# The third convolution of a token stage with its input as the stationary operand and 256 moving weight columns, and the last token norm folded into the output weights

## The reference, cut to what matters

```python
def tok(x):                                             # [b, 128, 64, 3]
    h = layernorm(x.reshape(b, t, j * 3), ln0_g, ln0_b).reshape(b, t, j, 3)
    h = relu(conv2d(h, conv1_w, conv1_b, ((2, 2), (1, 1))))
    h = layernorm(h.reshape(b, t, j * 3), ln0_g, ln0_b).reshape(b, t, j, 3)
    h = relu(conv2d(h, conv2_w, conv2_b, ((2, 2), (0, 0))))
    h = layernorm(h.reshape(b, t, j * 2), ln1_g, ln1_b).reshape(b, t, j, 2)
    h = relu(conv2d(h, conv3_w, conv3_b, ((2, 2), (0, 0))))   # 128 -> 256 token channels, 5 x 2 taps
    h = h.reshape(b, 2 * t, j)
    res = concatenate([h[:, :t, :], h[:, t:, :]], axis=2)     # [b, 128, 128]
    return layernorm(res, ln1_g, ln1_b) @ out_w + out_b       # -> [b, 128, 64]
# then: h + attention(layernorm(h)), whose logits are, for 8 heads and all pairs of the 128 tokens,
#   -sum_w |q[s, h, w] - k[t, h, w]| / 8                      over 64 w
# then: h + experts(layernorm(h)), one of 32 small experts for each token
```

## Time and profile before

| | before |
|---|---|
| median of 3 runs | 3468.23 us (3464.18 to 3468.46) |
| the profiled execution | 3481.97 us, span from first to last instruction 3480.2 us |
| PE busy | 3227.9 us (93%) |
| DVE busy | 3130.7 us (90%) |
| POOL busy | 2849.9 us (82%) |
| ACT busy | 2577.4 us (74%) |

### The profile page before, as it was taken

The page is one execution under the profiler, slowest core; times in us unless marked ns, Lnnn a source line. Parts: engine busy times, 40 slices in busy tenths (PEclk is TensorE's granted clock), DMA queues, the critical chain, the costliest instruction groups (busy, mean ns, idle before and its releaser), DMA issues. The chain is left out here.

```text
span 3480.2 us, 78005 instructions
## 1 busy us (share of the span) xinstructions
PE 3227.9 (93%) x23116; PEld 2461.7 (71%) x23116; DVE 3130.7 (90%) x4358; ACT 2577.4 (74%) x4378; POOL 2849.9 (82%) x2728
## 2 busy tenths in 40 slices
PE   8899999999999999999999999999999999999888
PEld 6677777776777777777777777767777777777655
DVE  5899999999999999999999999999999999999876
ACT  3777787777777777777777777777777777777763
POOL 3788888888888888888888888888888888888874
PEclk9999999999999999999999999999999999999988
DMA  6778777778777778777777777787777787777773
GB/s 136 152 156 161 154 158 158 153 154 166 155 152 158 153 153 166 156 156 153 156 157 158 157 157 154 154 165 153 157 158 153 155 163 157 155 155 153 157 152 70
DMA packets 199652, 534.96 MB, mean 154 GB/s; under 512 B 69142, under 2 KB 133398, under 8 KB 150968
## 3 DMA queue, kind: packets, MB, share of 16 engines
q0 software_dynamic: 73728, 492.86, 71.4%
q1 hardware_dynamic: 125880, 41.54, 5.9%
HBM read 10.93 MB, written 2.10 MB: 4 GB/s over the span
## 5 line engine op out<-in xcount | busy, mean ns | idle before, releaser
L925 DVE TENSOR_REDUCE S<-psU 128x16 f32<-128x1024 f32 x2216 | 2629.9, 1217 | 235.4 <-PE psU L487 220.9
L487 PE MATMUL psU<-flat,kT 99*128 99x256 bf16 x16384 | 2291.6, 275 | 189.9 <-DVE S L925 119.4
L712 ACT ACTIVATE absd<-psU 128x1024 f32<-128x1024 f32 x1880 | 1913.4, 1023 | 587.0 <-PE psU L487 575.9
L487 PEld LDWEIGHTS psU<-flat,kT 99*128 99x128 bf16 x16384 | 1498.0, 98 | 832.1 <-DVE S L925 316.8
L1183 POOL TENSOR_TENSOR absd<-absd 128x1024 f32<-128x1024 f32 (+2 forms) x512 | 1183.5, 2312 | 111.3 <-DMA absd<-absd 110.1
L1189 POOL TENSOR_TENSOR absd<-absd 128x512 f32<-128x512 f32 (+4 forms) x768 | 767.5, 999 | 60.2
L1171 POOL DMA_DIRECT2D absd<-absd x512 | 454.0, 887 | 244.8 <-ACT absd L712 186.2
L499 PE MATMUL psC<-c1in,w 128*128 128x384 f32 (+1 forms) x930 | 314.3, 421 | 17.0 <-DVE c1in L969 16.9
L591 PE MATMUL psZ<-P,v 128*128 128x256 f32 x1024 | 279.1, 379 | 0.0
L936 DVE TENSOR_REDUCE S<-absd 128x64 f32<-128x512 f32 (+4 forms) x512 | 264.3, 516 | 1.3 <-POOL absd L1189 1.3
L518 PE MATMUL psC<-c3in,w 128*128 128x128 f32 x1240 | 245.8, 282 | 1.7 <-DVE c3in L969 1.7
(11 more groups left out here) (180 smaller groups left out, 2266.8 us busy)
## 6 DMA issues: line engine op xcount, KB each, us to landing
absd<-absd POOLq DMA_DIRECT2D x379, 1024.0 KB, 8.1
absd<-absd POOLq DMA_DIRECT2D x98, 768.0 KB, 6.5
flat<-qparts SPq DMA_DIRECT2D x3072, 8.0 KB, 4.0
absd<-absd POOLq DMA_DIRECT2D x35, 512.0 KB, 4.6
xin<-in_x SPq DMA_DIRECT2D x32, 192.0 KB, 6.4
flat<-pattern SPq DMA_DIRECT2D x4, 768.0 KB, 10.9
out_h<-result SPq DMA_DIRECT2D x32, 64.0 KB, 6.1
w<-in_w SPq DMA_DIRECT2D x1, 1280.0 KB
```

The source lines that it names most:

```text
L487: mm = nc.tensor.matmul(psU[:, slot % PLACES, m], kT[0:ROWS + 3, b, m, :], flat[0:ROWS + 3, half % HALVES, :, lo:lo + BLOCK], start=True, ...
L712: nc.scalar.activation(absd[:, c % GROUPS, :, u], psU[:, slot % PLACES].rearrange("p (n a) s w -> p n (a s w)", n=2), ACT.Abs).then_inc(a_ ...
L925: nc.vector.tensor_reduce(S[:, b, hd, SB * c:SB * c + SB], psU[:, slot % PLACES].rearrange("p a s w -> p s a w"), AX.XY, ALU.add, apply_ab ...
```

## The change

The operands of the third convolution swap roles. The input of a tap, c3in with the batch as its innermost dimension (64 positions x 2 batches = 128 columns), becomes the stationary operand, and the weights of both halves are the 256 moving columns: 10 matmuls, and one bf16 matmul of three rows that adds the bias, which the lead-in splits into three bf16 parts. So the convolution's output has its (position, batch) on the partitions. ACT applies relu and writes SBUF (res); PE transposes res back for the statistics and at the same time multiplies it by `wcentre`, which holds the output weights times gain, less their mean over the features, for each batch separately. What is left of the norm is one factor per token: DVE forms h = product x rstd + constant in two operations, one for each batch. ACT's norm, its gain and shift, and POOL's two products go. The positions change too: conv3 is spread over slots 76, 78, 81, 84, 86, 89, 92, 95, 97 and 100, its bias matmul stands at 103, relu at 106, transposes and product together at 111, statistics at 113, and h at 119. In the lead-in the smaller loads of gain, shift and output weights become twelve DMAs, and DVE makes the bias rows (`weigh_out`) and the folded weights (`fold`).

```diff
-TOK_ACT = Steps("copy relu1 relu2 relu3a relu3b norm0 norm1 turned")
+TOK_ACT = Steps("copy relu1 relu2 relu3")
...
-TOK_POOL = Steps("vara rstda varb rstdb varc rstdc vard rstdd meand shiftd")
+TOK_POOL = Steps("vara rstda varb rstdb varc rstdc vard rstdd")
...
-TOK_AT = dict(copy=3, a=7, conv1=14, len1=22, b=47, conv2=56, len2=10, c=67, conv3=76, len3=33, d=112, turn=121,
-              out=126, root=0, gap=4)
+TOK_AT = dict(copy=3, a=7, conv1=14, len1=22, b=47, conv2=56, len2=10, c=67, conv3=76, len3=30, d=113, turn=111,
+              out=118, root=0, gap=4)
...
+        for b in range(2):
+            for hf in range(2):
+                here, there = slice(b, T, 2), slice(hf * J, hf * J + J)
+                weights += [(ln1g_col[here, hf:hf + 1], a["ln1g_col"][there, :]),
+                            (ln1b_col[here, hf:hf + 1], a["ln1b_col"][there, :]), (wout[here, hf, :], a["wout"][there, :])]
...
-                for n in spread(slot, TOK_AT["conv3"], TOK_AT["len3"], 20):
+                for n in spread(slot, TOK_AT["conv3"], TOK_AT["len3"], 11):
...
-                    hf, m = n // 10, n % 10
-                    dy, dx = m // 2, m % 2
-                    mm = nc.tensor.matmul(z[:, 0:2 * T].rearrange("p (b a j) -> p b a j", b=2, a=2)[:, :, hf, :],
-                                          w3[:, m, hf * T:hf * T + T], c3in[:, :, dy:dy + J, dx],
-                                          start=(m == 0), stop=(m == 9))
...
+                    if n < 10:
+                        mm = nc.tensor.matmul(z[:, 0:2 * T], c3in[:, n % 2, n // 2:n // 2 + J, :].rearrange("p j b -> p (j b)"), w3[:, n, :],
+                                              start=(n == 0), stop=False)
+                    else:
+                        nc.tensor.matmul(z[:, 0:2 * T], ones_row[:, :], b3rows[:, :], start=False, stop=True).then_inc(by_pe, 1)
                 if slot == TOK_AT["turn"]:
-                    pe.wait_ge(by_act, TOK_ACT.after(q, "norm1"))
-                    for b in range(2):
-                        mm = nc.tensor.transpose(z[:, b * T:b * T + T], resn[:, b, :], ident[:, :])
+                    pe.wait_ge(by_act, TOK_ACT.after(q, "relu3"))
+                    for hf in range(2):
+                        mm = nc.tensor.transpose(z[:, hf * T:hf * T + T], res[:, hf, :], ident[:, :])
                     mm.then_inc(by_pe, 1)
-                if slot == TOK_AT["out"]:
-                    pe.wait_ge(by_act, TOK_ACT.after(q, "turned"))
-                    for b in range(2):
-                        mm = nc.tensor.matmul(z[:, b * LAT:b * LAT + LAT], resT[:, b, :], wout[:, :],
-                                              start=True, stop=True)
+                    for hf in range(2):
+                        mm = nc.tensor.matmul(z[:, 2 * T:2 * T + 2 * LAT], res[:, hf, :], wcentre[:, hf, :],
+                                              start=(hf == 0), stop=(hf == 1))
                     mm.then_inc(by_pe, 1)
...
+                    if name == "c":
+                        to = c3in[:, :, 2:2 + J, b].rearrange("p w j -> p j w")
+                        y = z[:, b * n:b * n + n].rearrange("p (j w) -> p j w", w=2)
+                        nc.vector.scalar_tensor_tensor(to, y, rstd[name][:, b:b + 1],
+                                                       bb[:, :].rearrange("p (j w) -> p j w", w=2),
+                                                       ALU.mult, ALU.add).then_inc(by_dve, 1)
+                        continue
...
-                    nc.vector.tensor_tensor(h[:, :, :], z[:, 0:2 * LAT].rearrange("p (b w) -> p b w", b=2),
-                                            bout[:, :, :], ALU.add).then_inc(by_dve, 1)
+                    dve.wait_ge(by_pool, TOK_POOL.after(q, "rstdd"))
+                    for b in range(2):
+                        nc.vector.scalar_tensor_tensor(h[:, b, :], z[:, 2 * T + b * LAT:2 * T + b * LAT + LAT],
+                                                       rstd["d"][:, b:b + 1], cout[:, :], ALU.mult, ALU.add).then_inc(by_dve, 1)
```

More of the change, by code:

```diff
@@ L658, in first @@
                         pe.wait_ge(ones, ONES)
+                        pe.wait_ge(split, 7)
+                    if s == TOK_AT["conv3"] + TOK_AT["len3"]:
+                        pe.wait_ge(folded, 4)
+                        for n, w in enumerate((wgain, wshift)):
+                            for hf in range(2):
+                                mm = nc.tensor.matmul(psZ[:, n * LAT:n * LAT + LAT], average[:, :], w[:, hf, :],
+                                                      start=(hf == 0), stop=(hf == 1))
+                        mm.then_inc(averaged, 1)
+                    if s == TOK_AT["turn"]:
+                        pe.wait_ge(folded, 11)
                     tok(0, s, psL, lead_pe, lead_act, lead_dve)
@@ L1001, in tok @@
                 if slot == TOK_AT["d"]:
[L1002 to L1003 removed]
+                    dve.wait_ge(by_pe, TOK_PE.after(q, "out"))
+                    stats(z[:, 0:2 * T].rearrange("p (f b) -> p b f", b=2), "d", by_dve, after("d"))
                 if slot == TOK_AT["out"] + 1:
@@ L1113, in first @@
                         dve.wait_ge(ones, ONES)
-                    if s == TOK_AT["out"]:
-                        dve.wait_ge(loaded, LOADED)
+                    if s == TOK_AT["turn"] - 1:
+                        fold()
                     tok(0, s, psL, lead_pe, lead_act, lead_dve, lead_pool)
+                    if s == TOK_AT["c"] + TOK_AT["gap"]:
+                        weigh_out()
                     if s == TOK_AT["a"] + TOK_AT["gap"]:
```

103 lines of the change are left out of this document (65 added, 38 removed).

## The result

| | before | after |
|---|---|---|
| median | 3468.35 us (4 runs, 3464.18 to 3473.89) | 3495.86 us (4 runs, 3493.28 to 3497.04) |
| profiled execution | 3481.97 us, span 3480.2 | 3493.28 us, span 3491.4 |
| PE, DVE, ACT, POOL busy | 3227.9, 3130.7, 2577.4, 2849.9 us | 3221.0, 3145.9, 2525.8, 2836.1 us |

The change makes the kernel slower (ratio 1.0074, 95% interval 1.006 to 1.0087); the medians lie 27.5 us apart where 25 were forecast. The sum came out right; of its larger parts only h did, and one part was missing.

A forecast was written before the change was run, and what follows sets the result against it. No engine is full; PE and DVE nearly are and hold each other, so DVE's read of slot 127 counts. 0.72 us a pair over 30 iterations (21.6) plus 3.7 lead-in make 25: 3468.2 + 25 = 3493 us, range 3460 to 3508.

The forecast's parts named there:

- reads late through slots 86 to 97 and the rows for slot 116: Convolution matmuls in the PE-bound stretch delay DVE's reads, so SP sends slot 116's rows later: 0.25 us a pair.
- h behind slot 119: Two DVE operations in a stretch without a pause, where one was free in the seam's gap: 0.42 us (0.35 to 0.5).
- strided c3in: DVE's writes to c3in with 8-byte steps between columns cost 0 to 0.22 us more a pair; 0.05 taken.
- steady iteration: Three per-pair terms, 0.25 + 0.42 + 0.05 = 0.72 us, lengthen the iteration from 105.4 to 106.1 us.
- lead-in: Before the first unit: weight operations on DVE and the order delay h of pair 0; net 3.7 us (1 to 8).
- sum: Whole execution: 21.6 us over 30 iterations and 3.7 in the lead-in, 25 us slower.
- The convolution on PE: Twenty 0.23 us matmuls (4.6 us) become ten of 0.44 (4.4) plus a bias matmul: PE gains nothing worth counting.
- The step to slot 116: Rows land 0.25 us later; 0.7 to 0.85 us of transposes and product stay covered by the 1.05 us DMA wait.
- rival (b): Strides to c3in cost their upper end: 5 us more, 3498, or 3505 with the statistics' reads; chance 0.08.
- frees nothing: Work PE loses behind slots 121 and 126 gives no time back, since DVE has no pause there.
- (d): Relief pays: ACT's 1.5 us and PE's 0.64 shorten DVE's waits by 0.5 to 0.7 us a pair; 3468, chance 0.17.
- A premise: Iteration 30, without token stage, still takes 105.0 us, so work taken out of the token stage comes back as waiting.

The follow-up runs named there:

- experiment 2: Changed kernel with the two operations for h moved back behind slot 127, the product left where the change put it: 3509.74 us, ratio 1.0124.
- experiment 4: Changed kernel with weights laid out by the host, 9 transfers instead of 19 and none of single elements: 3502.29 us, ratio 1.01.
- Experiments 5 to 7: 5: kernel before, output product cut to one column, 3496.79 us; 6: changed kernel, product and h back at the seam, 3484.85; 7: changed kernel, zero matmuls there, 3492.4.
- the second profile of the kernel before: The kernel before, unchanged, run and profiled again: 3468.75 us, ratio 1.0007, its profiled execution 3468.93 us.
- the fastest kernel: Changed kernel with the experiments' remedies combined, zero matmuls in the last two iterations, and pair 0's norm ahead of pair 1's convolution input: 3462.07 us, ratio 0.9975.

## Why the prediction was right, and where only its sum was

| term | forecast | measured |
|---|---|---|
| reads late through slots 86 to 97 and the rows for slot 116 | +0.25 us a pair | -0.04 us at the read of slot 116, -0.19 from slot 117 on |
| h behind slot 119 | +0.42 | +0.38 (experiment 2) |
| strided c3in | +0.05 (0 to 0.22) | +0.02 on DVE, 0.01 at the reads behind it |
| steady iteration | +0.72 | +0.20 (105.40 to 105.60) |
| lead-in | +3.7 (1 to 8) | +10.1 |
| half-clock stretches at the seam | not in the sum | 2 in the trace, 12.6 us against the same iterations of before |
| sum | 25 | 27.5 (medians) |

*The convolution on PE.* Right: 0.43 us from start to start, and no gain although the group's busy time fell from 245.8 to 186.7 us. The pauses before slots 91, 93 and 95 grew from 0.80 + 0.42 + 0.75 = 1.97 to 2.16 us, the one before slot 108 vanished, as forecast; new ones of 0.45 and 0.32 us came before slots 110 and 112, which were not.

*The step to slot 116* failed. I let the rows of q for slot 116 land as much later as SP sends them. They are sent about 0.3 us later and are no longer waited for. With the lump of 0.66 us on PE, slots 112 to 115 are read 0.9 to 1.0 us later than before, so that PE comes later to slot 116, and the rows are there: the last of their three transfers takes 7.4 us from issue to landing in the iteration of the earlier trace rows and 5.3 us in the same iteration of the changed kernel, and over iterations 3 to 28 it lands 95.5 us behind slot 0's read before the change and 93.7 us behind it after, in the median. So the wait of 1.05 us on PE, and 0.91 on DVE, took up the lump, and the read of slot 116 came out at the old time. In these traces a landing is not a fixed delay behind its issue. What made this one shorter was not tried.

*h* was sized right. From slot 121 on DVE's reads are 0.20 us later than before, which is 0.38 less the 0.19 us that it had gained up to slot 118, 0.04 of it at slot 116 and the rest where its pause before slot 118 fell from 0.52 to 0.38 us. The wait before slot 1 grew to 0.70 us, not to the 0.79 forecast.

*c3in.* An operation takes 434 ns against 347 in the kernel before, two a pair, and their union grew from 0.61 to 0.71 us. But these are durations, and the next operation starts before they end. The kernel before, then the changed one:

```profile
1703.62 0.61 DVE L969 SCALAR_TENSOR_TENSOR c3in<-psC,rstdc,ln1b 128x128 f32<-128x128 f32 x2 [0.62 <-POOL rstdc L1203]
1704.14 1.22 DVE L925 TENSOR_REDUCE S<-psU 128x16 f32<-128x1024 f32 x1
```

```profile
1718.16 0.71 DVE L982 SCALAR_TENSOR_TENSOR c3in<-psC,rstdc,ln1b 128x128 f32<-128x128 f32 x2 [0.62 <-POOL rstdc L1264]
1718.70 1.20 DVE L935 TENSOR_REDUCE S<-psU 128x16 f32<-128x1024 f32 x1
```

From start to the next start they cost 0.52 and 0.54 us, and the reads from slot 75 to slot 87 stand where they stood, within 0.01 us on DVE. The forecast of 0.05 was near enough; 0.10, as the busy time has it, would be too much. The statistics read psC in steps of 8 bytes at 285 ns, against 286 before. So rival (b) was wrong on the write and on the read. By the Trainium skill's rule in "SBUF — State Buffer" on cachelines the write pays a penalty; the trace agrees by duration, with 87 ns more for 128 columns, and shows almost none of it as time lost to DVE.

*The lead-in* was mis-sized where no row had a price. DVE waited 3.69 us for the last weights; SP took 7.1 us to issue the two b3 transfers of single elements, and only 3.2 us came back without them (experiment 4). The eleven operations took 3.4 us, at the upper end of the estimate (2 to 3.3). So the convolution began at 35.63 us and not near 31.7. PE had been idle for 6.79 us, the clock stood at 0.50 for 6.8 us from 32.3 on, and the convolution took 6.27 instead of 4.49 us. The second convolution and, behind pair 1's input as forecast, h of pair 0 were moved on by both: h came at 52.87 us, 11.4 us later instead of 5.8.

*What was missing.* The prediction said that what PE loses behind slots 121 and 126 "frees nothing". It frees nothing, but it takes away the work that held the clock up. Experiments 5 to 7 show this from three sides: with the product thinned in the kernel before, the clock falls at the seam; with the product put back in the changed kernel, or zeros in its stead, it stays. The sum was right to 2.5 us by luck: 15.6 us too much in the iterations (0.52 x 30) met 6.4 too little in the lead-in and 12 of clock. Of the rivals, (d) was the best on the steady iteration, for a reason that it did not name.

*A premise* was read from a stretch with the lower clock in it. That iteration 30, without a token stage, "still" takes 105.0 us stands in the earlier trace rows beside a mean clock of 0.97. It takes 102.2 us in the second profile of the kernel before and 100.5 us in the changed kernel's, so not all of the token stage's work comes back as waiting.

## What to carry to other kernels

Where the longest engine loses work at a place where it also waits, look at the granted clock of the stretch behind it, not only at the waits. Where 0.44 us of matmuls stand, in front of the seam or behind slot 111, made 25 us between experiments 2 and 6, more than any other term of the change. Compare two traces only when the half-clock stretches of both are listed: the first profile of the kernel before was 13 us over the second one, nearly all of it from the clock in its first and last two iterations. And the first unit's chain in a lead-in is worth a walk backwards: taking pair 0's norm ahead of pair 1's input, which does not feed the first unit, was worth 6.7 us. And price an operation by the distance to the next start, on DVE as on PE: the strided write to c3in looks four to five times as dear by its busy time.

## What the runs showed of the hardware

The clock fell without any long pause of PE. This is PE in front of the fall at 912.9 us in the changed kernel:

```profile
907.13 1.10 PE L506 MATMUL psU<-flat,kT 99*128 99x256 bf16 x8 [0.27 <-DVE S L935]
908.84 2.34 PE L506 MATMUL psU<-flat,kT 99*128 99x256 bf16 x16 [0.61 <-DVE S L935]
911.69 0.61 PE L506 MATMUL psU<-flat,kT 99*128 99x256 bf16 x4 [0.52 <-ACT absd L737]
912.75 2.62 PE L506 MATMUL psU<-flat,kT 99*128 99x256 bf16 x12 [0.45 <-DVE S L935]
```

Four pauses of 0.27 to 0.61 us in 6 us, with units between them, and from 912.9 on the granted clock is 0.50: 12 matmuls last 2.62 us, where the same 12 last 1.48 us in the kernel before. In the kernel before the pauses of this place are 0.22, 0.28 and 0.45 us, with transposes and product among the units, and neither trace has a fall there in iterations 1 to 30. Every iteration of the changed kernel has the pattern, and only two fell; in the other kernels that showed it there were two to four. Even the fastest kernel, with the product back, has one of 17.1 us, which begins 1.1 us behind slot 0's read of iteration 2 (111.1 us), so the cure is not complete. The time of such a fall was 5.5 to 7.6 us, for 17.1 or 20.5 us at the lower level, while those that began some 11.8 us behind slot 0 in the two profiles of the kernel before lasted 3.4 us and cost 1.4 to 2. The Trainium skill, in "TensorE: Matmul & The Clock Gate", Part 1, says that a monitor of how busy PE has been sets the clock; the experiments agree. Why the clock came back after 3.4 us in one place and after 17.1 in the other, no run here tells apart.

Busy time and the distance from start to start barely show what was taken away. Product and next unit, in the kernel before and in that with one column:

```profile
1747.09 0.56 PE L531 MATMUL psC<-wout,resT 128*128 128x64 f32 x4
1747.48 0.60 PE L487 MATMUL psU<-flat,kT 99*128 99x256 bf16 x4
```

```profile
1756.06 0.50 PE L531 MATMUL psC<-wout,resT 128*128 128x1 f32 x4
1756.42 0.60 PE L487 MATMUL psU<-flat,kT 99*128 99x256 bf16 x4
```

0.56 and 0.50 us of busy time, 0.39 and 0.36 us to the next start: by time almost nothing was taken away, and the clock fell four times.
